# Audio tower on one core: a shared down product in three rounded products, routed weights loaded in place, gate and up in banks of their own, and 99 blocks

## The chip, the core and the metric

The kernel runs on one core of a Trainium2 chip. The metric is the device time of one execution in microseconds. A core has five engines with a queue each: PE (TensorE, matrix products; its loads of stationary operands are PEld), DVE (VectorE), ACT (ScalarE), POOL (GpSimd) and SP (SyncE, which issues DMA transfers). Engines run their own queue in order and wait for each other through semaphores.

## What is computed

The reference takes x of 16 sequences, 128 channels and 750 times. Three layers follow each other:

```python
# tokenizer: forward and backward moving average over time, then a projection 128 -> 256
ewma = (scan(x) + reversed_scan(x)) * 0.5
h = einsum('btc,dc->btd', ewma, W) + b
# two selective scans of 64 states along time
delta = softplus(x @ Wd + bd); u = x @ Wi + bi
h_t = exp(-delta * softplus(A_log)) * h_(t-1) + delta * u;  y = h_t @ Wo + bo
hidden = y + state @ Ws + bs
# mixture of experts over 12000 tokens: 16 experts in 4 groups of 4; each token keeps 2 groups, 4 experts
shared = (silu(x @ sg.T) * (x @ su.T)) @ sd.T                      # hidden size 512
routed = sum_e w_e * ((silu(x @ gate_e) * (x @ up_e)) @ down_e)    # 64 per expert
```

The scans are linear, and the kernel folds some weights into each other ahead of time. float32 accuracy is kept by splitting an operand into a rounded part (fp32r, "hi") and a rest ("lo") and adding three products: hi by hi, hi by lo and lo by hi.

## The kernel before

**Iterations and ticks.** The sequences are worked on in 8 pairs, one iteration each, of 24 ticks (`TICKS`), and a tail of 22 ticks. A tick holds one slot: a shared slot (`SHARED`: ticks 0 to 3, 7 to 10, 13 to 16) or a block slot (`ROUTED`: ticks 4 to 6, 11, 12, 17 to 23). Iteration q works the shared slots of pair q, and the blocks of tokens up to pair q-1. I call ticks 0 to 16 stretch A and ticks 17 to 23 stretch B of an iteration; B has seven block slots and no shared one.

**A shared slot** takes 500 tokens and a quarter of the shared hidden size. PE makes gate and up (12 products 500 wide, `shared_products`, L1593), ACT takes silu of gate (L868), DVE multiplies by up (`shared_hidden`, L1388), and three ticks later PE makes the down product (`shared_down`, L1656) in plain float32: 4 products in 8 records. After four such slots DVE adds the sum to the rows (`finish`, L1404).

**A block slot** takes 128 tokens that chose the same two groups. POOL gathers them through a list (L734), PE transposes them (L1635, `block_x`), ACT and DVE split them (L880, L1408), and PE makes gate and up (`block_products`, L1616): for each of the two groups six products 512 wide, gate in the first half of a bank and up in the second. ACT takes silu of both at once (`block_silu`, L873), after all twelve. DVE multiplies by up and by the weight of the token, one expert at a time (`block_hidden`, L1397, eight instructions 64 wide). PE transposes the result (L1643), ACT and DVE split it again (L891, L1414), PE makes the down product in 12 products 256 wide (`block_down`, L1674), ACT copies the sum (L886) and POOL adds it to the output (L745).

**Lists of blocks.** A block needs 128 tokens of one class of two groups. After the first pair only 6 full blocks are sure to be there, but 12 slots are run; entries without a token are masked by their index. The loop makes `KB` = 12 blocks in each of seven iterations and `KE` = 22 in the tail, 106 in all.

**The chain** (`CHAIN`) is the work that leads a pair from x to its lists: the moving average (`ewma`, scans L1038 and L1045, then POOL L690 and L692), projection (`tok`, L1511), layer statistics, the two scans (`pre`, `ssm_*`; L829, L831 and L834 on ACT, L1110 on DVE), the parts of the state (`split`, L1115), the class row (L1123), residuals on POOL (L706), `y` (PE L1558, DVE L1137), second statistics (L1066 to L1074), transposes, router (L1567), lists and the table of blocks (`table`, L1355 to L1378). Each step names a tick for each engine, counted from tick 0 of its pair: DVE=-30.5 of pair q is tick 17.5 of iteration q-2. An event at a whole tick runs before the tick's block or shared work on ACT and DVE, one at a half in the middle of the tick. `PREPARE` holds the loading and folding of weights in the same way. Chain, block inputs and block hidden rows use two banks in turn (`ch_ps`), in the order in which PE comes to them.

**Order in a tick** before, on ACT: silu of the block one slot back, sum of the block four back (L886), input of the next block (L880), chain, silu of this shared slot, chain, hidden rows of the block two back (L891). On DVE: the shared product one slot back, the rest of the next block's input (L1408), `finish`, chain, the block's hidden rows one slot back, chain, the rest of the block two back (L1414).

**Buffers** that the change touches: `h_tok` and `h2` (rows of the pair ahead of `y` and after it), four `hid` buffers, `fw` (the forward scan, and between times the scratch of the router), `block_rows` (8, and at the start the raw routed weights), `ws1` with a zero half per sequence.

## Time and profile before

| what | us |
|---|---|
| three runs | 1447.79, 1443.96, 1449.68 (median 1447.79) |
| the profiled execution | 1445.21, its span 1443.4 |
| PE busy in the span | 1221.5 |
| DVE busy | 997.5 |
| ACT busy | 559.2 |
| POOL busy | 599.7 |

The profile lists what each engine did in one execution. A busy PE isn't PE at its full pace, since products overlap: what counts is the distance from one start to the next. The granted clock of PE was 0.916 of full speed over the span.

### The profile page before, as it was taken

Reading aid. Unit: us, or ns where it says so; the run is one execution under the profiler, and the core shown is the slowest. Engines: PE = TensorE matmul, PEld = TensorE weight load, DVE = VectorE, ACT = ScalarE, POOL = GpSimd, SP = SyncE. Lnnn points to the kernel's source line nnn. Section 1 sums busy time; section 2 is a strip of 40 time slices with the busy share of each in tenths; the row PEclk is TensorE's granted clock in tenths of the full one; section 3 lists DMA queues with packets and bytes.
Section 4 is the critical chain, followed back from the end, with each engine's and each line's share of the span. In section 5 each row is a group of like instructions: output and inputs, shape, how many; then the busy total and the mean of one; then the engine's idle time right before and its main releaser. Section 6 shows DMA issues by size and latency. Waiting matters only on the chain.

```text
span 1443.4 us, 22785 instructions
## 1 busy us (share of the span) xinstructions
PE 1221.5 (85%) x6476; PEld 1036.5 (72%) x6476; DVE 997.5 (69%) x2991; ACT 559.2 (39%) x925; POOL 599.7 (42%) x442
## 2 busy tenths in 40 slices
PE   4439948996899779996799879998699979999997
PEld 3328736884788658885688658886588868888886
DVE  6785895779548875779548885588647774665553
ACT  1523613651336423551235423463236523323332
POOL 2261163155422743146332635138341553265553
PEclk9559978998899999998899978998899999999999
DMA  3601112221221112221231112212122213123330
GB/s 73 154 27 58 32 25 79 48 45 37 39 71 41 32 43 56 68 43 33 47 81 41 32 37 43 70 38 42 37 63 49 46 42 69 40 37 58 48 36 9
DMA packets 86891, 71.00 MB, mean 49 GB/s; under 512 B 38654, under 2 KB 81471, under 8 KB 86776
## 3 DMA queue, kind: packets, MB, share of 16 engines
q0 software_dynamic: 23616, 25.52, 11.6%
q1 hardware_dynamic: 60928, 43.61, 10.6%
q8 instruction: 62, 1.02, 0.3%
q10 hardware_dynamic: 2232, 0.42, 0.2%
q14 instruction: 53, 0.43, 0.1%
HBM read 33.10 MB, written 39.52 MB: 50 GB/s over the span
## 4 chain that ended last, share of the span: by engine, by line
PE 56%; DVE 25%; issue 10%; POOL 3%; DMA 3%; ACT 2%; POOLq 0%; DVEq 0%; SPq 0%; ACTq 0%
PE gu_ps L1616 14%; PE gu_ps L1593 13%; PE d_ps L1674 9%; PE d_ps L1656 6%; DVE hid L1397 5%; PE ch_ps L1567 3%; PE ch_ps L1511 2%; PE ch_ps L1643 2%; DVE h L1404 1%; DVE h L1137 1%; DVE fw L1038 1%; DVE states L1115 1%; PE ch_ps L1635 1%; PE ch_ps L1521 1%; DVE ends L1030 1%
## 5 line engine op out<-in xcount | busy, mean ns | idle before, releaser
L745 POOL DMA_INDIRECT out_dram<-block_rows,entry x106 | 171.7, 1620 | 328.2 <-ACT block_rows L886 173.0
L1616 PE MATMUL gu_ps<-gu_hi,bx_hi 128*128 x424 | 193.0, 455 | 12.8 <-issue 12.7
L713 POOL DMA_INDIRECT lists<-listed,pos x96 | 131.8, 1373 | 164.7 <-DVE pos L1307 140.2
L1656 PE MATMUL d_ps<-down,hid 128*125 128x256 f32 x768 | 191.6, 395 | 0.0
L1397 DVE SCALAR_TENSOR_TENSOR hid<-gu_ps,entry,hid 128x64 f32<-128x64 f32 x848 | 171.7, 276 | 8.0 <-ACT hid L873 7.1
L1616 PE MATMUL gu_ps<-gu_hi,bx_lo 128*128 x424 | 176.1, 415 | 0.0
L1616 PE MATMUL gu_ps<-gu_lo,bx_hi 128*128 x424 | 175.4, 414 | 0.0
L1656 PEld LDWEIGHTS d_ps<-down,hid 128*125 128x125 f32 x768 | 147.9, 198 | 22.8
L873 ACT ACTIVATE hid<-gu_ps 128x512 f32<-128x512 f32 x106 | 63.4, 598 | 231.9 <-PE gu_ps L1616 231.8
L734 POOL DMA_INDIRECT block_rows<-token_rows,entry x106 | 112.5, 1061 | 64.5 <-issue 35.5
L1408 DVE TENSOR_TENSOR bx_lo<-ch_ps,bx_hi 128x256 fp32r<-128x256 f32 x106 | 44.6, 421 | 131.5 <-ACT bx_hi L880 127.9
L1674 PE MATMUL d_ps<-dr_hi,hid_hi 128*128 x424 | 125.8, 297 | 6.5 <-DVE h L1404 6.4
L891 ACT ACTIVATE hid_hi<-ch_ps 128x512 fp32r<-128x512 f32 x106 | 63.3, 597 | 151.6 <-PE ch_ps L1643 149.4
L1674 PE MATMUL d_ps<-dr_lo,hid_hi 128*128 x424 | 120.4, 284 | 0.0
L1674 PE MATMUL d_ps<-dr_hi,hid_lo 128*128 x424 | 119.9, 283 | 0.0
L1616 PEld LDWEIGHTS gu_ps<-gu_hi,bx_hi 128*128 128x128 f32 x424 | 85.3, 201 | 31.8 <-issue 18.8
L1414 DVE TENSOR_TENSOR hid_lo<-ch_ps,hid_hi 128x512 fp32r<-128x512 f32 x106 | 72.6, 685 | 47.8 <-ACT hid_hi L891 47.8
L1616 PEld LDWEIGHTS gu_ps<-gu_lo,bx_hi 128*128 128x128 f32 x424 | 85.1, 201 | 21.2
L1616 PEld LDWEIGHTS gu_ps<-gu_hi,bx_lo 128*128 128x128 f32 x424 | 85.9, 203 | 12.6
L868 ACT ACTIVATE hid<-gu_ps 128x500 f32<-128x500 f32 x96 | 56.2, 589 | 91.8 <-PE gu_ps L1593 90.8
L1674 PEld LDWEIGHTS d_ps<-dr_hi,hid_hi 128*128 128x128 f32 x424 | 81.0, 191 | 10.7 <-issue 9.0
L886 ACT ACTIVATE block_rows<-d_ps 128x256 f32<-128x256 f32 x106 | 40.8, 385 | 121.0 <-PE d_ps L1674 121.0
(273 smaller groups left out, 3006.8 us busy)
## 6 DMA issues: line engine op xcount, KB each, us to landing
token_rows<-xn SPq DMA_DIRECT2D x24, 500.0 KB
out_dram<-h SPq DMA_DIRECT2D x24, 500.0 KB
t<-rstd_scratch SPq DMA_DIRECT2D x24, 250.0 KB, 4.0
x_in<-in_x_dram SPq DMA_DIRECT2D x15, 375.0 KB, 3.4
entry<-lists SPq DMA_DIRECT2D x106, 8.0 KB, 2.5
block_rows<-token_rows,entry POOLq DMA_INDIRECT x106, 2.8
out_dram<-block_rows,entry POOLq DMA_INDIRECT x106, 3.8
lists<-listed,pos POOLq DMA_INDIRECT x96, 2.7
```

Of the source, the lines that this page charges most:

```text
L713: pool.indirect_dma_start(out=lists, out_offset=bass.IndirectOffsetOnAxis(pos[:, arg:arg + 1], 0), in_=listed[:, arg, :], in_offset=None). ...
L734: pool.indirect_dma_start(out=block_rows[u], out_offset=None, in_=token_rows[0:there, :], in_offset=bass.IndirectOffsetOnAxis(entry[n % UE ...
L745: pool.indirect_dma_start(out=out_rows[0:there, :], out_offset=bass.IndirectOffsetOnAxis(entry[n % UE][:, ID:ID + 1].bitcast(U32), 0), in_ ...
L868: inc(act.activation(hid[g % 4][:, 0:TT], gu_ps[:, 2 * (g % 2), 0:TT], ACT.Silu), "silu_done")
L873: inc(act.activation(hid[g % 4].rearrange("p (g h) -> p g h", g=2), gu_ps[:, 2 * (g % 2):2 * (g % 2) + 2, 0:GH], ACT.Silu), "silu_done")
L891: inc(act.activation(hid_hi[g % 2][:], ch("bh", 0, n), ACT.Copy), "b_hi")
L1397: last = dve.scalar_tensor_tensor(h, up, entry[n % UE][:, e:e + 1], h, ALU.mult, ALU.mult)
L1414: inc(dve.tensor_tensor(hid_lo[g % 2][:], ch("bh", 0, n), hid_hi[g % 2][:].bitcast(F32), ALU.subtract), "b_lo")
L1593: last = pe.matmul(bank, w[:, k, ms], xx[:, k, :], start=(k == 0 and q == 0), stop=(k == KD - 1 and q == 2))
L1616: last = pe.matmul(gu_ps[:, 2 * (g % 2) + q, :], a[n % 2][:, k, :], w[:, k, bass.ds(of, 1), :].rearrange("p g h -> p (g h)"), start=(k == ...
L1656: last = pe.matmul(d_ps[0:TP, j, :], hid[g % 4][:, tc], down[:, m, :], start=(m == 0 and j % 2 == 0), stop=(m == M - 1), skip_group_check= ...
L1674: last = pe.matmul(d_ps[:, 2 * (n % 2), :], a[g % 2][:, m * P:(m + 1) * P], rows_[:, bass.ds(of, 1), half * D:(half + 1) * D].rearrange("p ...
```

## The change

- **99 blocks.** The iterations take 0, 6, 12, 12, 11, 12, 12 and 12 blocks, and the tail 22. The slots that come free (ticks 4, 5, 6, 11, 12 and 17 of iteration 1, tick 4 of iteration 4) hold chain steps only.
- **Shared down** in 12 products 256 wide of `hid_hi`, `hid_lo`, `down_hi` and `down_lo`. ACT makes `hid_hi` (`shared_hi`) and DVE `hid_lo` (`shared_lo`, both of its inputs in SBUF) at the end of the tick two after the slot's own, and `shared_down` waits for that.
- **Banks.** Block gate goes to one bank and block up to another, in 24 products 256 wide. ACT takes silu in the slot's own tick, once gate is there. DVE multiplies up by the weights, in its bank (one instruction 512 wide), and then `hid` by that (one more).
- **ACT's order:** the next block's input first, then the sum, the chain and silu.
- **Routed weights** go from DRAM straight to the place of their lower part; their split moves from ticks ahead of tick 0 to ticks 1.4 to 11.4 of iteration 0.
- **Buffers.** Rows are kept in one of two `h` by parity, in place; three `hid`, six `block_rows`, and `route_t` for the router's scratch; three waits on `fw` fall away. `ws1` is half as large.
- **ACT tables** for Exp are loaded ahead of the waits of `ssm_log` and `ssm_decay`.
- **Ticks.** Most steps have other ticks, and `EARLY` gives nine of them others in iterations 0 and 1.

```diff
-    ("ewma", 0, dict(SP=-32.0, DVE=-30.5, POOL=-29.0, ACT=-28.5)),
-    ("ewma_back", 0, dict(DVE=-29.5)),
+    ("ewma", 0, dict(SP=-32.0, DVE=-33.5, POOL=-29.0, ACT=-28.5)),
+    ("ewma_back", 0, dict(DVE=-32.0)),
...
-    (-16.4, "routed", 0),
+    (1.4, "routed", 0),
...
-    taken = 0
     for q in range(1, NP):
-        taken = min(taken + KB, full(q))
-    KE = (B * T - NCLS) // P + NCLS - taken
-    NB = KB * (NP - 1) + KE
+        first.append(first[-1] + take[-1])
+        take.append(min(KB, full(q) - first[q]))
+    first.append(first[-1] + take[-1])
+    KE = (B * T - NCLS) // P + NCLS - first[NP]
...
+                    act.preload_act_table(ACT.Exp)
...
-            def block_silu(g):
-                wait(act, "prod_mm", done(g))
+            def silu(g, n):
+                wait(act, "half_mm", done(g))
                 hidden_is_free(g)
-                inc(act.activation(hid[g % 4].rearrange("p (g h) -> p g h", g=2),
-                                   gu_ps[:, 2 * (g % 2):2 * (g % 2) + 2, 0:GH], ACT.Silu), "silu_done")
+                inc(act.activation(hid[g % 3][:, 0:n], gu_ps[:, 2 * (g % 2), 0:n], ACT.Silu), "silu_done")
+
+            def shared_hi(pair, n, g):
+                wait(act, "hid_done", done(g))
+                wait(act, "down_mm", done(g - 2))
+                inc(act.activation(hid_hi[g % 2][:, 0:TT], hid[g % 3][:, 0:TT], ACT.Copy), "s_hi")
...
-                if slot(g - 1)[0] == "B":
-                    block_silu(g - 1)
+                if slot(g + 1)[0] == "B":
+                    block_x(slot(g + 1)[1], g + 1)
...
-                for e in range(2 * EG):
-                    h = hid[g % 4][:, e * H:(e + 1) * H]
-                    up = gu_ps[:, 2 * (g % 2) + e // EG, GH + e % EG * H:GH + (e % EG + 1) * H]
-                    last = dve.scalar_tensor_tensor(h, up, entry[n % UE][:, e:e + 1], h, ALU.mult, ALU.mult)
-                inc(last, "hid_done")
+                up = gu_ps[:, 2 * (g % 2) + 1, :].rearrange("p (e h) -> p e h", h=H)
+                if part == 0:
+                    wait(dve, f"entry_in{n % UE}", 16 * (n // UE + 1))
+                    wait(dve, "prod_mm", done(g))
+                    w = entry[n % UE][:, 0:2 * EG].unsqueeze(2).broadcast_to([P, 2 * EG, H])
+                    inc(dve.tensor_tensor(up, up, w, ALU.mult), "up_weighed")
+                else:
+                    h = hid[g % 3].rearrange("p (e h) -> p e h", h=H)
+                    wait(dve, "up_weighed", n + 1)
+                    wait(dve, "silu_done", done(g))
+                    inc(dve.tensor_tensor(h, h, up, ALU.mult), "hid_done")
...
+            def shared_lo(pair, n, g):
+                wait(dve, "s_hi", s_count(pair, n))
+                inc(dve.tensor_tensor(hid_lo[g % 2][:, 0:TT], hid[g % 3][:, 0:TT], hid_hi[g % 2][:, 0:TT].bitcast(F32),
+                                      ALU.subtract), "s_lo")
...
-                wait(pe, "hid_done", done(g))
+                wait(pe, "s_lo", s_count(pair, n))
...
-                    last = pe.matmul(d_ps[0:TP, j, :], hid[g % 4][:, tc], down[:, m, :],
-                                     start=(m == 0 and j % 2 == 0), stop=(m == M - 1), skip_group_check=True)
+                    for q, (a, w) in enumerate(((hid_hi, down_hi), (hid_hi, down_lo), (hid_lo, down_hi))):
+                        last = pe.matmul(d_ps[0:TP, j, :], a[g % 2][:, tc], w[:, m, :],
```

On DVE, around tick 17 of iteration 4, before: the last rows of the table of blocks, the parts of the state (`states`), the moving average of the pair two ahead (`ends`, and the scan that writes `fw`), and the first `y` (the row that writes `h`).

```order
922 L1378 TENSOR_SCALAR table<-fw 1x12
923 L1115 TENSOR_TENSOR states<-t,states 64x750 x2
924 L1030 TENSOR_SCALAR ends<-x_in 128x2
925 L1038 SCALAR_TENSOR_TENSOR fw<-c,ends,x_in 128x750
926 L1408 TENSOR_TENSOR bx_lo<-ch_ps,bx_hi 128x256
927 L1137 TENSOR_TENSOR h<-ch_ps,h_tok 125x512
928 L1143 BN_STATS stats<-h 125x6 x2
929 L1397 SCALAR_TENSOR_TENSOR hid<-gu_ps,entry,hid 128x64 x8
930 L1045 SCALAR_TENSOR_TENSOR x_in<-c,ends,x_in 128x750
```

The same place now:

```order
961 L1136 TENSOR_TENSOR states<-t,states 64x750 x2
962 L1384 TENSOR_TENSOR route_t<-route_t,step_c 1x66
963 L1386 TENSOR_REDUCE route_t<-route_t 1x11
964 L1387 TENSOR_SCALAR table<-route_t 1x11
965 L1384 TENSOR_TENSOR route_t<-route_t,step_c 1x66
966 L1386 TENSOR_REDUCE route_t<-route_t 1x11
967 L1387 TENSOR_SCALAR table<-route_t 1x11
968 L1427 TENSOR_TENSOR hid_lo<-hid,hid_hi 128x500
969 L1406 TENSOR_TENSOR gu_ps<-gu_ps,entry 128x512
970 L1421 TENSOR_TENSOR bx_lo<-ch_ps,bx_hi 128x256
971 L1152 TENSOR_TENSOR h<-ch_ps,h 125x512
```

The states now stand ahead of the table's last six rows (five more of the table stand a tick earlier), both scans have left for ticks 14.5 and 16, and a shared `hid_lo` and the product by the weights have come in.

On ACT, at ticks 20 and 21 of iteration 4, before: silu of a block (`hid`), the sum of an older one (`block_rows`), and the input of the next (`bx_hi`).

```order
470 L891 ACTIVATE hid_hi<-ch_ps 128x512
471 L873 ACTIVATE hid<-gu_ps 128x512
472 L886 ACTIVATE block_rows<-d_ps 128x256
473 L880 ACTIVATE bx_hi<-ch_ps 128x256
474 L852 ACTIVATE x_hi<-ch_ps 128x500
```

And now:

```order
504 L910 ACTIVATE hid_hi<-ch_ps 128x512
505 L899 ACTIVATE bx_hi<-ch_ps 128x256
506 L905 ACTIVATE block_rows<-d_ps 128x256
507 L888 ACTIVATE hid<-gu_ps 128x512
508 L872 ACTIVATE x_hi<-ch_ps 128x500 x2
```

The input of the next block has moved ahead of the sum and of silu.

## Rows read from the trace of the kernel before

**Rows 1.** Windows by tick: stretch, length, busy time (instructions), clock, DMA.

```profile
core 0: us, PE busy (x) PEld busy (x) DVE busy (x) ACT busy (x) POOL busy (x), PEclk, DMA share, GB/s
0.00:119.60 119.60, 51.82 (x206) 42.98 (x207) 92.36 (x204) 37.45 (x48) 43.62 (x34) 0.66 0.34 79
119.60:181.40 61.80, 59.31 (x288) 49.32 (x288) 45.15 (x140) 33.94 (x45) 9.44 (x7) 0.97 0.16 47
181.40:232.90 51.50, 25.61 (x120) 22.14 (x119) 43.12 (x91) 9.23 (x16) 30.63 (x22) 0.67 0.13 32
232.90:319.90 87.00, 84.33 (x453) 71.64 (x451) 61.49 (x202) 47.52 (x71) 25.64 (x21) 1.00 0.23 59
319.90:394.10 74.20, 56.06 (x272) 45.62 (x271) 55.56 (x141) 17.79 (x34) 38.40 (x28) 0.84 0.19 41
725.20:816.70 91.50, 89.36 (x498) 76.89 (x496) 63.29 (x209) 49.44 (x76) 30.87 (x23) 1.00 0.25 55
816.70:892.50 75.80, 56.50 (x272) 46.50 (x271) 55.62 (x141) 17.79 (x34) 38.45 (x28) 0.84 0.19 40
1149.80:1201.70 51.90, 43.30 (x236) 35.50 (x235) 37.00 (x123) 15.39 (x31) 29.63 (x24) 0.97 0.20 42
1321.20:1423.60 102.40, 102.40 (x629) 89.11 (x629) 54.21 (x213) 39.02 (x84) 51.66 (x39) 1.00 0.30 41
```

**Rows 2.** Chain that ended last, in the tail: start, us, what.

```profile
1419.11 1.40 PE gu_ps L1616 x6
1420.51 0.44 PE ch_ps L1643 x4
...
1422.34 1.44 PE d_ps L1674 x12
```

**Rows 3.** The same chain in stretch A of iteration 4, a shared down.

```profile
744.97 1.73 PE d_ps L1656 x8
```

**Rows 4.** Groups by form, whole span: count, busy us, mean ns, idle before.

```profile
L1397 DVE SCALAR_TENSOR_TENSOR hid<-gu_ps,entry,hid 128x64 f32<-128x64 f32 x848 | 171.7, 276 | 8.0 <-ACT hid L873 7.1
L1414 DVE TENSOR_TENSOR hid_lo<-ch_ps,hid_hi 128x512 fp32r<-128x512 f32 x106 | 72.6, 685 | 47.8 <-ACT hid_hi L891 47.8
L891 ACT ACTIVATE hid_hi<-ch_ps 128x512 fp32r<-128x512 f32 x106 | 63.3, 597 | 151.6 <-PE ch_ps L1643 149.4 <-issue 2.1
L1102 DVE TENSOR_TENSOR t<-t 128x750 f32<-128x750 f32 x16 | 15.0, 935 | 1.9 <-ACT t L831 1.1
```

**Rows 5.** DVE's timeline in stretch B of iteration 4.

```profile
818.58 2.19 DVE L1367 TENSOR_TENSOR fw<-kth,upto_b 1x72 f32<-1x72 f32 x1
...
823.51 1.90 DVE L1115 TENSOR_TENSOR states<-t,states 64x750 fp32r<-64x750 f32 x2
825.44 2.63 DVE L1030 TENSOR_SCALAR ends<-x_in 128x2 f32<-128x2 f32 x1
828.11 1.78 DVE L1038 TENSOR_TENSOR_SCAN fw<-c,ends,x_in 128x750 f32<-128x750 f32 x1
...
839.97 3.38 DVE L1074 TENSOR_TENSOR mv<-halves 125x4 f32<-125x4 f32 x1
```

**Rows 6.** POOL's timeline in the same stretch.

```profile
818.80 1.87 POOL L706 TENSOR_TENSOR h_tok<-h_tok,rows 125x512 f32<-125x512 f32 x1
...
825.53 2.50 POOL L706 TENSOR_TENSOR h_tok<-h_tok,rows 125x512 f32<-125x512 f32 x2
...
840.82 2.49 POOL L706 TENSOR_TENSOR h_tok<-h_tok,rows 125x512 f32<-125x512 f32 x2
```

**Rows 7.** Who waited for whom, whole span: us, times, longest.

```profile
DVE bx_lo L1408 <- ACT bx_hi L880: 127.9, 58, 4.9
```

**Rows 8.** Chain that ended last, stretch B of iteration 0.

```profile
213.84 7.18 DMA out_dram<-h
```

**Rows 9.** The same chain ahead of tick 0.

```profile
46.22 1.28 ACT L829
...
54.75 3.85 DVE t L1110
...
64.27 5.13 DMA hid<-L_ffn_shared_down_w_dram
```

More of the change, by code:

```diff
@@ new lines @@
+    ("class_row", 0, dict(PE=-7.0, DVE=-7.5)),
+    ("residual", 4, dict(POOL=-2.5)),
+    ("split", (1, 1), dict(ACT=-6.0, DVE=-7.0)),
+    ("residual", 5, dict(POOL=-2.0)),
+    ("y", (0, 0), dict(PE=-5.5, DVE=-6.0)),
+    ("y", (0, 1), dict(PE=-5.0, DVE=-4.5)),
+    ("ln2_stats", 0, dict(DVE=-4.5, POOL=-4.5)),
+    ("y", (1, 0), dict(PE=-4.5, DVE=-4.5)),
+    ("ln2_norm", 0, dict(DVE=-3.5, ACT=-3.5)),
+    ("y", (1, 1), dict(PE=-4.0, DVE=-4.0)),
+    ("ln2_norm", 1, dict(DVE=-1.5, ACT=-0.5)),
@@ new lines @@
+    ("table", 0, dict(DVE=15.0)),
+    ("list", 10, dict(POOL=19.5)),
+    ("table", 1, dict(DVE=16.5)),
+    ("table", 2, dict(DVE=16.5)),
+    ("route_weights", 0, dict(DVE=13.0)),
+    ("table", 3, dict(DVE=17.5)),
+    ("list", 11, dict(POOL=20.0)),
+)
+EARLY = {
+    (1, "tok", 5): dict(DVE=-24.5),
+    (1, "table", 3): dict(DVE=19.5),
+    (1, "list", 11): dict(POOL=22.0),
+    (1, "list", 6): dict(POOL=16.5),
+    (0, "route_top", 0): dict(DVE=10.5),
+    (0, "route_groups", 1): dict(DVE=7.5),
+    (0, "route_marks", 0): dict(DVE=12.0),
+    (1, "list", 8): dict(POOL=19.5),
+    (1, "table", 0): dict(DVE=14.0),
+}
@@ L144 @@
+    (11.4, "routed", 5),
+    (-7.7, "shared", 5),
+    (-9.5, "routed_loads", 0),
+    (-8.5, "routed_loads", 1),
+    (-7.5, "routed_loads", 2),
+    (-6.5, "routed_loads", 3),
+    (-5.5, "routed_loads", 4),
+    (-4.5, "routed_loads", 5),
 )
@@ L582, in prepare @@
                                      w.rearrange("(m p) c -> p m c", p=P)).then_inc(S[f"w_shared{n}"], 16)
-                    for n in range(3):
-                        routed_chunk(n)
-                elif what == "routed" and 1 <= n <= 3:
-                    routed_chunk(n - 1 + 3)
+                elif what == "routed_loads":
+                    load_routed(n)
                 elif what == "shared" and n == KD:
@@ L709, in chain @@
                     if arg == 0 and pair:
-                        for n in range(KB * (pair - 1), KB * pair):
+                        for n in range(first[pair], first[pair + 1]):
                             wait(pool, f"entry_in{n % UE}", 16 * (n // UE + 1))
@@ L725, in fetch @@
                 u = n % U
-                if n % KB == 0:
+                if n == first[iteration[n]]:
                     for t in range(NT):
@@ L739, in add_to_out @@
                 u = n % UO
-                if n % KB == 0:
+                if n == first[iteration[n]]:
                     for t in range(NT):
@@ L832, in chain @@
                 elif step == "ssm_decay":
+                    act.preload_act_table(ACT.Exp)
                     wait(act, "delta_done", 2 * pair + arg + 1)
@@ L1336, in blocks_from @@
                 last = pair == NP - 1
-                n0, k = KB * pair, KE if last else KB
+                n0, k = first[pair + 1], take[pair + 1]
                 fl, got, many, by = tb
@@ L1578, in banks_of_slot @@
             def banks_of_slot(g):
-                if slot(g)[0] == "S" and slot(g - 2)[0] == "S":
-                    wait(pe, "silu_done", done(g - 2))
-                else:
-                    wait(pe, "hid_done", done(g - 2))
+                wait(pe, "silu_done", done(g - 2))
             def shared_products(pair, n, g, amid, groups):
```

385 lines of the change are left out of this document (184 added, 201 removed).

## The prediction

> **What bounds the kernel now.** I read the windows first [rows 1], cut at the first gate product of a tick; the cuts fall at the ends of stretches A and B, so that every row is one kind of work. Three regimes are to be seen. In the tail 21 block slots take 102.40 us, 4.88 each, and PE is busy for all of it at full clock: PE is the bound. In stretch A of iteration 4 (twelve shared and five block slots) PE is busy for 89.36 of 91.50 us, again the bound, and DVE has 63.29 of work, so a cover of 28. In stretch B PE is busy for only 56.50 of 75.80 us, at a clock of 0.84, and DVE for 55.62: seven block slots, 34 us at the tail's pace, take 76. Neither is full; they wait for each other through the chain. Without averages and projection for a pair two ahead, as in iteration 6, the same stretch takes 51.90 us. Ahead of tick 0 lie 119.60 us in which DVE is busy for 92.36, and iteration 0, which has no blocks, takes 61.80 and 51.50.
>
> Then the chain and the timelines. DVE's rows in B [rows 5] tell why the first `y` is late: the table, from 818.58 to the states at 823.51, then `ends` and a scan from 825.44 to 829.89. Three rows there are far longer than their size: 2.19 us for 72 numbers, 2.63 for two columns, 3.38 for four columns. Each lies over a residual of POOL [rows 6] and ends with it. Last, the waits [rows 7]: DVE waited for the block input from ACT 58 times, 127.9 us; ACT makes it behind silu of the previous block and a sum.
>
> **The change part by part**, against the profiled execution's 1445.2 us. That lies 2.6 below the median of the runs, which is inside their spread.
>
> *Six blocks of iteration 1.* Five leave ticks 4 to 12. Iteration 1 takes 87.00 there, and iteration 0, which has the same chain steps and no blocks, 61.80 [rows 1]: -25. The sixth leaves tick 17, a block at the tail's 4.88: -5. Together -30; at least -18, if the chain waits as long without them. One more leaves iteration 4: -5.
>
> *Shared down.* Eight records take 1.73 us [rows 3]; twelve products 256 wide take 1.44 in a block's down [rows 2], with the same stationary loads. That is -0.29 for each of 96. All lie in stretch A, where PE sets the pace, but iteration 0's are on a chain of waits, so 84 count: -24.
>
> *Block gate and up.* Twelve products 512 wide take 2 x 1.40; 24 of 256 take 2 x 1.44 [rows 2]: +0.08 for each of 99, +8.
>
> *Stretch B of iterations 1 to 5.* Ahead of the first `y` the table (4.9) and `ends` with its scan (4.4) go, and two `hid_lo` come, each of 500 columns where 750 take 935 ns [rows 4], 0.62: -8.1. The scan back, of the same length as the 1.78 [rows 5], leaves a tick in which PE waits too, and I count half: -0.9. ACT's order takes one silu out from ahead of each block input, a pass of 512 columns as the 597 ns of row L891: seven times 0.6, -4.2. `block_hidden` takes 171.7 / 106 = 1.62 now and should take twice one pass of 512 from a bank, 0.685 [rows 4], 1.37: seven times, -1.7. The sum is -14.9, and I take -14, which leaves 62 us: five times, -70. Below that, the stretch can't go under seven slots and its own chain on PE, for which I take the 56.5 it is busy now, part of it at half clock: -19. Above, half of it, -7, if the waits only change places. Iteration 6 has no scans there: -6.
>
> *Stretch A with more for DVE and ACT.* DVE gets twelve `hid_lo` (7.4), two scans (3.6), and some 1.5 of table, 12.5 us a stretch; ACT gets twelve passes of 0.59, 7.1 on 49.44. The 28 us of DVE's cover shrink to about 13 of the 88 that PE then needs. Queued behind `hid_lo` on DVE is the next tick's shared product and so PE's banks; behind the new wait of `shared_down` on PE stands the whole next slot. I charge +3 for each of seven iterations, +21; nothing at the low end, +8 each at the high end.
>
> *Ahead of tick 0.* The splits of the routed weights leave. Now they hold up the load of the shared down weights (5.13 us, behind a buffer wait of SP) and lie over a scan that takes 3.85 on DVE; an Exp table of 1.28 sits on the chain twice [rows 9] and goes ahead of the wait. Of this sum, 5.1 + 2.0 (a scan of the same 750 columns takes 1.78) + 2.6, I take all, -10. No row shows what a direct load costs while it lies beside the pair's rows; its bounds are nothing and its own 5.13.
>
> *Iteration 0.* `y` waits for a transfer of 7.18 us, since `h2` must be stored first [rows 8]; with two `h` it doesn't: -7. Two Exp loads, -2.6. Against it come the six splits on ACT and POOL and `hid_lo`: +3. Together -7.
>
> *At nothing:* `ws1` by halves (one more wait of PE in a step that occurs once a pair), six `block_rows` (gathered up to six slots ahead), three `hid`, whose third is needed free one slot sooner: all hidden by the slot's other work as long as DVE is not a whole tick late; 1 us a pair if it is.
>
> The sum: -30 - 5 - 24 + 8 - 70 - 6 + 21 - 10 - 7 = -123, so 1322 in a profiled execution and 1325 as a median.
>
> **A rule that speaks against the change.** Row by row, three instructions of DVE were held by a residual of POOL for about 2, 2.5 and 3.2 us [rows 5, 6]. `shared_lo` reads two operands from SBUF, where a block's rest reads one from PSUM; two of them per iteration come at ticks 17 and 18, where residuals start at tick 17.5. If each is held for a pair of residuals, 2.5 us, that is +5 in each of seven iterations, and on the chain.
>
> The Trainium skill's page "SBUF — State Buffer", section "SBUF: two separate sides", says just this: a DVE instruction with two inputs in SBUF and a GpSimd instruction that reads SBUF lock each other out for a whole instruction. The trace agrees as far as the three rows go.
>
> **The rivals.**
>
> 1. *DVE becomes late (rival).* The lock costs the 35 us above, or stretch A +8 instead of +3, also 35: 1360, and with half the gain in B 1395. For it: DVE would be busy for 76 of 88 us in A, and PE now waits for DVE in every slot instead of in block slots only. Against: the residuals run in stretch B, and A has little of POOL but transfers. Chance 0.22.
> 2. *Stretch B falls to PE's own work.* 56.5 instead of 62 in five iterations, -27, and A pays nothing, -21: 1277. For it: iteration 6 does it at 51.90. Against: averages and projections stay, and the three held rows may stay too. Chance 0.18.
> 3. *The new ticks do nothing.* Only the seven blocks leave and the rest cancels: 1448 - 35 = 1413. Chance 0.06.
> 4. *Slower: `shared_down` waits for DVE.* PE's queue stops at the end of each tick until DVE has ended the tick before. Everything else saves 123 + 21 = 144 us, so 84 shared slots would have to lose 1.7 us each to bring the kernel back to where it was, and 1.8 for slower by over 0.5%. DVE's slack is 13 us over 17 ticks, 0.8 a tick, and for a loss of 1.8 a tick it would have to be late almost always. Chance 0.04, at 1460.
>
> The forecast itself, 1300 to 1355, has 0.5. About 0.5% is what a measurement of this kernel can tell from no change. Faster by more than that is 0.95, the same 0.02, slower 0.03. The range takes in the cases 1 and 2 with their bounds: 1270 to 1390.
>
> **What would show it.** Iteration 1 shorter by 30 or more; tail slots at 4.96 instead of 4.88; the shared down at 1.44 and not 1.73; stretch B of iterations 2 to 5 at 62; stretch A at 88 to 94, with DVE at 76 in it; two instructions of 0.68 in place of eight; the block input no longer first among DVE's waits; tick 0 at 110. Wrong would be: a stretch A over 97 (rival 1 or 4, told apart by whether DVE or PE's wait for `s_lo` is long), a B under 57 (rival 2) or over 70 (rival 3), or 256-wide products that take more than 0.12 us from start to start in the new order.

## The result, and the profile after

Four runs of the changed kernel gave 1388.3 to 1393.0 us, median 1389.8; four of the kernel before beside them gave 1447.4. The ratio is 0.961, with a 95% interval of 0.958 to 0.963: 4% faster, where 8.5% was forecast. Windows with the same cuts and columns as [rows 1]: ahead of tick 0, iteration 0, A and B of iteration 1, A and B of 4, B of 6, 21 slots of the tail.

```profile
0.00:106.10 106.10, 50.33 (x206) 42.41 (x207) 82.65 (x197) 33.28 (x43) 25.44 (x27) 0.66 0.37 90
106.10:230.50 124.40, 93.33 (x455) 80.32 (x454) 100.86 (x243) 56.76 (x79) 53.77 (x32) 0.78 0.13 38
230.50:307.20 76.70, 64.98 (x351) 54.65 (x350) 63.06 (x182) 44.38 (x62) 19.40 (x12) 0.93 0.16 46
307.20:366.80 59.60, 44.60 (x315) 42.23 (x314) 42.08 (x85) 15.50 (x30) 26.95 (x21) 0.86 0.13 33
684.40:774.20 89.80, 84.54 (x551) 75.56 (x549) 69.45 (x193) 51.56 (x81) 35.37 (x25) 0.98 0.27 61
774.20:838.00 63.80, 51.17 (x368) 48.74 (x368) 45.96 (x94) 18.67 (x36) 33.91 (x24) 0.89 0.18 38
1090.60:1143.10 52.50, 42.72 (x331) 40.52 (x331) 34.19 (x75) 16.73 (x33) 23.60 (x19) 0.97 0.16 35
1266.70:1370.80 104.10, 104.10 (x882) 104.10 (x882) 48.30 (x84) 38.57 (x83) 50.10 (x38) 1.00 0.30 44
```

Against [rows 1]: 13.5 less ahead of tick 0, 11 more in iteration 0 (113.3 there), 10 and 15 less in the stretches of iteration 1, 12 less in B of iteration 4. A of iteration 4 lost a block and only 1.7 us (b_99, the kernel before with 99 blocks, loses 0.9 there). A tail slot is 104.10 / 21 = 4.96, where it was 4.88. The waits of the changed kernel that have to do with new code:

```profile
ACT hid L888 <- DVE hid_lo L1427: 59.7, 24, 4.1
DVE hid_lo L1427 <- ACT hid_hi L893: 39.7, 23, 4.1
DVE h L1152 <- POOL h L725: 25.4, 6, 6.0
PE d_ps L1684 <- DVE hid_lo L1427: 23.6, 10, 5.8
PE d_ps L1703 <- DVE h L1417: 19.6, 9, 2.8
```

The wait of [rows 7] is out of the first places. New are waits for `hid_lo` of a shared slot (L1427), and one of DVE for POOL's residual (L1152 for L725).

### The profile page after: what moved, and what is told of

The parts are those of the page before. It is cut to its first block, busy times and chain, and to the rows that moved or that the text cites. A ratio compares the mean times of both kernels' runs of the same rounds, so it can differ in the third digit from the quotient of the medians.

```text
span 1389.0 us, 25702 instructions
## 1 busy us (share of the span) xinstructions
PE 1170.6 (84%) x7838; PEld 1073.6 (77%) x7838; DVE 981.0 (71%) x2424; ACT 591.6 (43%) x989; POOL 590.9 (43%) x428
## 4 chain that ended last, share of the span: by engine, by line
PE 48%; issue 17%; DVE 16%; POOL 12%; ACT 3%; DMA 3%; SPq 1%; POOLq 0%; DVEq 0%; ACTq 0%
PE gu_ps L1642 14%; PE gu_ps L1617 9%; PE d_ps L1703 9%; POOL lists L732 5%; PE ch_ps L1594 3%; PE d_ps L1684 3%; POOL block_rows L753 3%; PE ch_ps L1533 2%; PE ch_ps L1670 2%; POOL h L725 2%; PE ch_ps L1543 1%; DVE fw L1054 1%; POOL out_dram L764 1%; PE ch_ps L1662 1%; DVE hid_lo L1427 1%
## 5 line engine op out<-in xcount | busy, mean ns | idle before, releaser
L888 ACT ACTIVATE hid<-gu_ps 128x512 f32<-128x512 f32 (+1 forms) x195 | 115.3, 592 | 368.2 <-PE gu_ps L1642 226.8
L1642 PE MATMUL gu_ps<-gu_hi,bx_hi 128*128 x792 | 240.3, 303 | 14.5 <-issue 14.5
L1642 PE MATMUL gu_ps<-gu_lo,bx_hi 128*128 x792 | 230.9, 292 | 0.0
L1642 PEld LDWEIGHTS gu_ps<-gu_hi,bx_hi 128*128 128x128 f32 x792 | 157.7, 199 | 23.4 <-issue 22.8
L1642 PEld LDWEIGHTS gu_ps<-gu_hi,bx_lo 128*128 128x128 f32 x792 | 157.9, 199 | 0.4
L1642 PEld LDWEIGHTS gu_ps<-gu_lo,bx_hi 128*128 128x128 f32 x792 | 157.2, 199 | 0.0
L1684 PE MATMUL d_ps<-down_hi,hid_hi 128*125 128x256 f32 x384 | 118.1, 308 | 23.9 <-DVE hid_lo L1427 23.6
L1684 PE MATMUL d_ps<-down_hi,hid_lo 128*125 128x256 f32 x384 | 112.1, 292 | 0.0
L1684 PE MATMUL d_ps<-down_lo,hid_hi 128*125 128x256 f32 x384 | 111.9, 291 | 0.0
L1684 PEld LDWEIGHTS d_ps<-down_hi,hid_hi 128*125 128x125 f32 x384 | 75.8, 197 | 31.4 <-DVE hid_lo L1427 31.1
L1427 DVE TENSOR_TENSOR hid_lo<-hid,hid_hi 128x500 fp32r<-128x500 f32 x96 | 70.2, 731 | 40.6 <-ACT hid_hi L893 39.7
```

What stands on the lines that cost most here:

```text
L888: inc(act.activation(hid[g % 3][:, 0:n], gu_ps[:, 2 * (g % 2), 0:n], ACT.Silu), "silu_done")
L1427: inc(dve.tensor_tensor(hid_lo[g % 2][:, 0:TT], hid[g % 3][:, 0:TT], hid_hi[g % 2][:, 0:TT].bitcast(F32), ALU.subtract), "s_lo")
L1642: last = pe.matmul(gu_ps[:, 2 * (g % 2) + half, q * GH:(q + 1) * GH], a[n % 2][:, k, :], w[:, k, bass.ds(of, 1), half * GH:(half + 1) * GH ...
L1684: last = pe.matmul(d_ps[0:TP, j, :], a[g % 2][:, tc], w[:, m, :], start=(m == 0 and q == 0 and j % 2 == 0), stop=(m == M - 1 and q == 2), ...
```

## The experiments

Three theories for what was missing stood at the start. Theory 1: POOL's queue holds up stretch B. Theory 2: POOL's splits of the routed weights, moved into iteration 0, hold DVE there. Theory 3: the new waits for `hid_lo` and the DVE instruction behind them. The rival to all is that the terms were wrong in size and no new wait matters.

Eighteen kernels were run in five groups, each with its own runs of the kernel before (medians 1445.8 to 1450.0), so ratios compare best. "C" is the changed kernel with both product edits undone.

| kernel | median us | ratio to before | 95% interval |
|---|---|---|---|
| changed | 1389.8 | 0.961 | 0.958-0.963 |
| b_99: before, 99 blocks | 1424.4 | 0.984 | 0.981-0.986 |
| a_down32: changed, float32 shared down | 1369.4 | 0.947 | 0.946-0.949 |
| a_banks_old: changed, old block gate/up | 1376.4 | 0.951 | 0.949-0.953 |
| a_both = C | 1355.5 | 0.937 | 0.932-0.941 |
| a_pe_no_lo | 1380.9 | 0.954 | 0.950-0.959 |
| a_hid_free | 1388.7 | 0.960 | 0.955-0.964 |
| a_no_lo | 1369.3 | 0.942 | 0.939-0.946 |
| a_pool_first | 1409.1 | 0.974 | 0.971-0.976 |
| a_pool2 | 1411.3 | 0.975 | 0.971-0.980 |
| c_oldchain | 1432.3 | 0.986 | 0.982-0.991 |
| c_scans_back | 1369.0 | 0.942 | 0.937-0.946 |
| c_tables_back | 1359.6 | 0.940 | 0.938-0.942 |
| c_y_back | 1425.3 | 0.985 | 0.983-0.987 |
| c_ssm_back | 1372.7 | 0.947 | 0.944-0.950 |
| c_routed_back | 1357.4 | 0.934 | 0.931-0.938 |
| a_lists_back | 1362.3 | 0.942 | 0.938-0.946 |
| c_lists_back | 1337.9 | 0.924 | 0.923-0.926 |
| c_lists_late | 1321.7 | 0.912 | 0.909-0.915 |

Lengths from the profiled executions, cut as above; each column adds up to its span. The profiled executions of a_down32 and C are 5 and 3 us faster than their medians.

| stretch | before | b_99 | changed | a_down32 | C | c_lists_late |
|---|---|---|---|---|---|---|
| ahead of tick 0 | 119.6 | 121.1 | 106.1 | 106.2 | 104.8 | 105.4 |
| iteration 0 | 113.3 | 116.3 | 124.4 | 113.8 | 112.3 | 116.2 |
| iteration 1 | 161.2 | 136.5 | 136.3 | 124.1 | 126.6 | 122.0 |
| A of 2 to 5 | 365.5 | 365.4 | 369.1 | 363.1 | 360.6 | 362.2 |
| B of 2 to 5 | 299.5 | 296.1 | 260.2 | 260.5 | 257.9 | 236.6 |
| iteration 6 | 142.6 | 147.6 | 147.1 | 146.5 | 143.0 | 138.0 |
| iteration 7 | 119.4 | 119.8 | 123.5 | 125.6 | 124.1 | 120.4 |
| tail | 122.2 | 121.6 | 122.3 | 122.3 | 120.6 | 121.5 |

**99 blocks alone.** The edit is `take.append(min(KB, full(q) - first[q]))` and what follows from it.

> The kernel before with 99 blocks instead of 106 and nothing else of the change. The prediction gives -30 for iteration 1 and -5 for iteration 4: 1412, ratio 0.976. The changed kernel's iteration 1 came out only 24.9 us shorter, though other edits also act there. If the chain waits as long without blocks, iteration 1 gives -18 and the kernel 1424 (0.984). A result near 1412 says that the terms of the blocks were right and that what is missing lies elsewhere.

1424, the number of the lower bound, but not by its mechanism: iteration 1 is 24.7 shorter and not 18, 14 in A and 11 in B, and iteration 4 another 3. Of this 5 come back in iteration 6 and 3 in iteration 0.

**The two product edits, one by one and together.** The cuts show the products alone; silu, DVE's instructions and ACT's order of a block go back with them in a_banks_old, the buffers in a_down32.

```diff
 a_down32
-        for q, (a, w) in enumerate(((hid_hi, down_hi), (hid_hi, down_lo), (hid_lo, down_hi))):
-            last = pe.matmul(d_ps[0:TP, j, :], a[g % 2][:, tc], w[:, m, :], ...)
+        last = pe.matmul(d_ps[0:TP, j, :], hid[g % 4][:, tc], down[:, m, :], ...)
 a_banks_old
-        last = pe.matmul(gu_ps[:, 2 * (g % 2) + half, q * GH:(q + 1) * GH], ...)
+        last = pe.matmul(gu_ps[:, 2 * (g % 2) + q, :], ...)
```

> The changed kernel with before's plain float32 shared down (eight instructions, no rounded part and no rest, four hid buffers, one down load). By the prediction it loses 0.29 us for each of 96 shared slots on PE and gets back the charge of 3 us for each stretch A: about +24 - 21, 1393. Theory 3 (DVE and ACT carry the new rest too late, PE waits for hid_lo in every shared slot): 1365 to 1380, with stretch A at or under 90. Theory 1 (POOL's queue is what keeps stretch B long) expects B unchanged at 64 to 65 and the kernel at 1390 to 1410.

> The changed kernel with before's gate and up of a block: products 512 wide into two banks, silu after all twelve, eight DVE instructions a block that read entry and both halves, and the wait for DVE ahead of the products. The prediction puts this edit at -2.9 for each of five stretches B on the chain (-14), another -3 a stretch for ACT's order, and +8 for PE's narrower products: undoing it gives about 1390 + 30 - 8, 1412. If the order of ACT and DVE in a block hides all of it, the undone edit gives -8, 1382.

> The changed kernel with both product edits undone: plain float32 shared down with four hid buffers, and before's 512-wide block gate and up. One alone gave 1369.4 and the other 1376.4, where the changed kernel stands at 1389.8, so 20.4 and 13.4 were lost to them. If the two losses are of different places (the first in iterations 0 and 1, the second in stretches A and in the tail), they add: 1356. If both are the same wait for DVE seen twice, the second undoing gives little: 1366 or more.

Both undoings make the kernel faster, by 20.4 and 13.4 us, and they add: 1355.5 where 1356 was expected. Theory 3 holds for the first. The table above says where that loss lies: 10.6 in iteration 0, 12.2 in iteration 1, 6 in the four stretches A, none in B. The second lies elsewhere. Up to 8 of its 13.4 are the width, as forecast (4.96 a tail slot and not 4.88), and between the profiled executions of a_down32 and C, 3.5 us lie in iteration 6, 2.5 each in the stretches A and B of 2 to 5, 1.7 in the tail. PE's timeline in A of iteration 3 says why the twelve narrow products saved nothing. First the changed kernel, then the eight float32 products of a_down32: the first start of the down, and the start of the next product.

```profile
600.23 0.39 PE L1684 MATMUL d_ps<-down_hi,hid_hi 128*125 128x256 f32 x1
...
601.75 0.39 PE L1617 MATMUL gu_ps<-x_hi,gate_hi 128*128 128x500 f32 x1
...
608.50 0.36 PE L1703 MATMUL d_ps<-dr_hi,hid_hi 128*128 x1 [2.83 <-DVE h L1417]
```

```profile
574.39 1.89 PE L1681 MATMUL d_ps<-down,hid 128*125 128x256 f32 x8
...
575.93 0.58 PE L1615 MATMUL gu_ps<-x_hi,gate_hi 128*128 128x500 f32 x1
...
580.36 0.36 PE L1699 MATMUL d_ps<-dr_hi,hid_hi 128*128 x1 [0.93 <-DVE h L1417]
```

From start to start a shared down takes 1.52 as three rounded products and 1.54 in float32; over all slots after iteration 1 the medians are 1.50 and 1.54. The 1.73 of [rows 3] is a duration up to the end of the last product, which overlaps the next one's start. In the kernel before, the same down of iteration 4 starts at 744.80 and what follows at 746.34, 1.54 later too:

```profile
744.80 1.89 PE L1656 MATMUL d_ps<-down,hid 128*125 128x256 f32 x8
746.34 0.59 PE L1616 MATMUL gu_ps<-gu_hi,bx_hi 128*128 x1
```

The third row of each of the two timelines shows PE waiting for DVE's `finish` in the same place, 2.83 against 0.93: PE is no longer what sets the end of this tick. The windows of that A, of the changed kernel and of a_down32, agree: PE is busy for 2 us less and the stretch is longer.

```profile
527.20:620.20 93.00, 88.08 (x594) 79.04 (x592) 70.88 (x195) 53.13 (x85) 35.85 (x26) 1.00 0.28 61
```

```profile
500.60:592.40 91.80, 90.06 (x558) 79.85 (x556) 66.17 (x188) 48.35 (x75) 36.53 (x25) 1.00 0.28 62
```

**Which part of the shared rest costs.** Three kernels take away one piece each.

```diff
 a_pe_no_lo
-                wait(pe, "s_lo", s_count(pair, n))
+                wait(pe, "s_hi", s_count(pair, n))
-  ((hid_hi, down_hi), (hid_hi, down_lo), (hid_lo, down_hi))
+  ((hid_hi, down_hi), (hid_hi, down_lo), (hid_hi, down_hi))
 a_hid_free
-                    wait(act, "s_lo", s_count(*was[1:]))
+                    wait(act, "s_hi", s_count(*was[1:]))
-                inc(dve.tensor_tensor(hid_lo[...], hid[...], hid_hi[...], ALU.subtract), "s_lo")
+                inc(dve.tensor_tensor(hid_lo[...], hid_hi[...], hid_hi[...], ALU.subtract), "s_lo")
 a_no_lo: the edits of both but for the last, and no shared_lo on DVE
```

> The changed kernel, where PE's third product of a shared down reads hid_hi once more and not hid_lo, and waits for ACT's hid_hi alone; DVE still computes hid_lo. So the product with the rest of the hidden is left out, at the same count and width of instructions. If PE's wait for DVE at the end of a tick is what costs the 20 us of the split shared down: 1370 to 1375. If it is DVE's time (0.67 a slot), or ACT's wait for DVE ahead of silu (a third hid buffer where four were): 1385 to 1390, unchanged.

> The changed kernel, where DVE's hid_lo of a shared slot is hid_hi minus hid_hi, so that hid is free once ACT has rounded it and silu of the slot three later doesn't wait for DVE; the rest of the hidden is thereby left out (it is zero), with DVE's and PE's instructions and PE's wait as they were. If ACT's wait for DVE ahead of silu (59.7 us, 24 times in the changed kernel) costs the 20 us: 1370 to 1375. If PE's own wait or DVE's time does: 1385 to 1390.

> The changed kernel without any hid_lo of a shared slot: DVE doesn't compute it, PE's third product reads hid_hi once more, ACT and PE wait for ACT's hid_hi alone. So the product with the rest of the hidden is left out; PE's count and width of instructions and ACT's work are as in the changed kernel. PE's wait for hid_lo alone gave 9 of the 20.4 us (1389.8 to 1380.9). If the rest is DVE's time, 0.67 in each of 96 slots: 1370 or less. If the rest is ACT's rounding pass and its place in ACT's queue: 1380.

ACT's wait, the longest in the list of waits, is worth nothing (0.960, inside the changed kernel's interval). PE's wait is worth 9 us, and DVE's instruction another 12, which brings the kernel to a_down32's 1369. That the two agree is in part chance: in the profiled execution of a_no_lo iteration 7 is 10 us longer than in the changed kernel, nearly all of it in B, so elsewhere it gains 31. The gaps of PE's weight loads for which the profile shows no wait are 8.0 us there and 4.5 in the changed kernel; the reason is open, so the 12 for DVE's instruction is a net figure. How the wait works is to be seen in the chain of the changed kernel in iteration 0:

```profile
152.44 2.25 DVE route_t L1292
...
155.02 0.93 DVE states L1136
...
156.48 0.93 DVE states L1136
...
157.44 0.69 DVE hid_lo L1427
158.18 2.92 PE d_ps L1684 x12
```

And the first two of the twelve in PE's timeline:

```profile
158.18 0.58 PE L1684 MATMUL d_ps<-down_hi,hid_hi 128*125 128x256 f32 x1 [5.79 <-DVE hid_lo L1427]
158.55 0.41 PE L1684 MATMUL d_ps<-down_lo,hid_hi 128*125 128x256 f32 x1
```

`hid_lo` stands at the end of DVE's tick, behind routing and `states`. PE has waited 5.79 us for it, with the whole next tick queued behind the down, and then takes 2.72 from start to start (2.92 to the end of the last), where it took 1.52 in stretch A. The products lie 0.21 apart there and 0.12 in stretch A, and the granted clock of these 2.72 us was 0.50, the lower of its two levels (1.2 of 2.4 GHz):

```profile
158.18:160.90 2.72, 2.72 (x13) 2.72 (x14) 1.15 (x9) 0.00 (x0) 0.00 (x0) 0.50 0.00 0
```

So PE came out of its wait at the lower level. In iterations 0 and 1 of a_down32 the granted clock is 0.84 and 0.94, in the changed kernel 0.78 and 0.90 (A and B of iteration 1: 0.93 and 0.86):

```profile
106.20:220.00 113.80, 89.76 (x408) 74.43 (x407) 93.79 (x231) 50.44 (x67) 51.26 (x32) 0.84 0.14 42
220.00:344.10 124.10, 107.84 (x616) 93.29 (x615) 93.64 (x254) 53.10 (x80) 44.65 (x32) 0.94 0.16 45
```

No run separates how much of the 23 us in these two iterations is the clock and how much the waits themselves.

**POOL's order, first try.** In stretch B of the changed kernel the first `y` waits for POOL's residuals, and they stand behind list transfers. I moved them up, and the first sum of averages with ACT's copy of it; in a_pool2 ACT's stays at -28.5.

```diff
-    ("ewma", 0, dict(SP=-32.0, DVE=-33.5, POOL=-29.0, ACT=-28.5)),
+    ("ewma", 0, dict(SP=-32.0, DVE=-33.5, POOL=-31.0, ACT=-30.5)),
-    ("residual", 0..2, dict(POOL=-6.5)),
+    ("residual", 0..2, dict(POOL=-7.0)),
```

> The changed kernel with POOL's order altered in two places alone: the first sum of averages (fw plus scan back) and ACT's copy of it 2 ticks earlier, and the first three residuals ahead of the list transfers 5 to 8. Theory 1 (in stretch B the first y and the block of the scan both wait for POOL, which works off twelve list transfers, gathers and adds without a gap): each of five stretches B falls by 3 to 6 us, 1360 to 1375, and POOL's share of the chain falls from 12% to under 8%. Rival (DVE and the two-way chain of PE and DVE keep B long, POOL is only the last one seen): within 5 us of 1390.

> The changed kernel with POOL's order altered alone (first sum of averages at -31, first three residuals ahead of the list transfers 5 to 8). The run before it had also moved ACT's copy of the averages ahead of ACT's copy of the states, and DVE then waited 9.5 us for the states in every stretch B. Theory 1: without that the first y no longer waits 3.15 us for POOL and the averages' transfer starts some 6 us earlier; each of five stretches B falls by 3 to 6 us, 1362 to 1376. Rival (the chain of DVE and PE sets the pace of B, POOL's place in it is taken by the next wait): 1385 to 1395.

Both lost about 20 us, and theory 1 seemed to fall. The rows of a_pool2 in B of iteration 4, POOL and then DVE, show what happened:

```profile
787.21 4.32 POOL L725 TENSOR_TENSOR h<-h,rows 125x512 f32<-125x512 f32 x3
790.94 2.31 POOL L709 TENSOR_TENSOR fw<-fw,x_in 128x750 f32<-128x750 f32 x1
804.06 1.80 POOL L711 TENSOR_TENSOR ew_lo<-fw,ew_hi 128x750 fp32r<-128x750 f32 x1 [10.82 <-ACT ew_hi L816]
```

```profile
788.27 5.78 DVE L1136 TENSOR_TENSOR states<-t,states 64x750 fp32r<-64x750 f32 x1 [1.99 <-ACT states L836]
...
817.86 0.69 DVE L1152 TENSOR_TENSOR h<-ch_ps,h 125x512 f32<-125x512 f32 x1 [5.54 <-POOL h L725]
```

The step that I moved has two halves, and the second waits for ACT, which comes to it later: POOL stood still for 10.82 us with all else behind it, the fourth residual among it. And the residuals now lay beside DVE's `states`, which took 5.78 where it takes 0.94. In a_pool_first ACT had moved as well, ahead of its copy of the states, and in the same stretch DVE waited 9.51 us for that; its B of 2 to 5 is 262.5, only 2 more than in the changed kernel, and most of its loss lies in the stretches A (6), ahead of tick 0 (4) and in iteration 0 (5), which I didn't follow up. These trials moved more than the one thing, and don't settle whether POOL holds up B. The lists, tried last, do.

**Where the rest of the gain comes from.** b_99 to C is 69 us that no product edit explains.

```diff
 c_oldchain: CHAIN of the kernel before, EARLY empty. The others put back one group of it:
 c_scans_back    ("ewma", 0): DVE=-33.5 -> -30.5;  ("ewma_back", 0): DVE=-32.0 -> -29.5
 c_tables_back   ("table", 0..3): DVE=15.0, 16.5, 16.5, 17.5 -> 16.0, 16.0, 17.0, 17.0; its two rows of EARLY
 c_y_back        ("y", (2, 0)): PE=-1.5 -> -3.0;  ("y", (2, 1)): PE=-0.5 -> -2.0;
                 ("logit", 0): PE=-2.0 -> -1.5; ln2_stats, ln2_norm, x2t and
                 the other y by 0.5 to 1.5 ticks
 c_ssm_back      pre, split, carry, ssm_*, class_row, spread
```

> On the same kernel (1355.5), the whole table of chain steps of the kernel before, so that what stays of the change is the 99 blocks, the routed weights loaded in place, two h buffers, six block_rows, ws1 by halves. The kernel before with 99 blocks alone stands at 1424. The prediction's terms for the table are -9.0 in five stretches B and -6 in iteration 6, and for the loads and the buffers -10 and -7: about 1406 if each is what I took it for. If the loads and buffers give all of the 69 us: 1360; if they give nothing: 1424.

> On the kernel with both product edits undone (1355.5), the scans of batch 0 (ends, scan, scan back) at their ticks of the kernel before, in stretch B ahead of the first y. The prediction gave 4.4 + 0.9 us of each of five stretches B to these two moves: 1355.5 + 26, 1382. Rival (the first sum of averages waits for POOL's place in its own queue, so the scan's tick is free within B): 1350 to 1362.

> On the kernel with both product edits undone (1355.5), the four table steps alone at their ticks of the kernel before (16, 16, 17, 17). The prediction gave the table's 4.9 us ahead of the first y to each of five stretches B: 1355.5 + 25, 1380, all of it in B. Rival (as with the scans, DVE has the time there, since the first y waits for POOL's residual): 1352 to 1362.

> On the same kernel, the steps y, second norm with its statistics, x2t and logit at their ticks of before. The prediction costed their moves at nothing. If the order around y is what shortened stretch B, by 9 us each: 1355.5 + 40, about 1395. If not, within 7 of 1355.

> On the same kernel, the projections, splits, carry, state scan with its logarithm and decay, class row and the spread of the norm's rows at their ticks of before. The prediction costed their moves at nothing. If they shortened B and the stretch ahead of tick 0: 1375 to 1400. If not, within 7 of 1355.

With the old table nothing is left of the 69: 0.986 stands beside 0.984 of b_99, one interval over the other. So the table of steps is worth 5.0% and loads and buffers nothing together: against b_99, c_oldchain has 9 less ahead of tick 0 and 9 more in iteration 0. Of the groups, the scans give 0.5% by the ratios, with intervals that overlap, and nothing in B of 2 to 5 (255.6 with them back, 257.9 in C). The steps of the table of blocks give 1.4 us in each of these B and take 5.6 in the first two iterations, where their two rows of `EARLY` went as well; together nothing that can be measured. Projections and splits give 1.1%, in iterations 0 and 1 and the stretches A; B would be 1 us shorter without their moves. The steps around `y` are worth nearly all: 4.8%. (The parts add up to more than 5.0%, since the lists, below, cost 1.2%; the ticks of routing, token projection and residuals weren't tried alone.) Iteration 3, A and B, of c_y_back and then of C:

```profile
532.20:624.70 92.50, 89.99 (x498) 76.57 (x496) 68.14 (x217) 49.28 (x76) 32.71 (x22) 1.00 0.25 55
624.70:700.40 75.70, 56.21 (x272) 46.79 (x272) 45.43 (x133) 17.74 (x34) 37.32 (x27) 0.84 0.21 45
```

```profile
499.10:590.10 91.00, 89.53 (x498) 76.78 (x496) 68.77 (x224) 49.32 (x76) 36.56 (x25) 1.00 0.26 56
590.10:655.00 64.90, 49.07 (x270) 41.65 (x271) 44.50 (x126) 17.34 (x34) 35.70 (x25) 0.89 0.20 46
```

DVE's work in B is the same to 1 us, and B differs by 10.8. The last third's `y` has left ticks 21 and 22 for 22.5 and 23.5, and its norm's statistics have left B for the next A, which doesn't grow (91.0 against 92.5). In c_y_back the two slots that start at ticks 21 and 22 take 14.7 and 13.5, in C 9.4 and 6.7, and the clock is 0.84 against 0.89.

**The routed weights.**

> On the same kernel (1355.5), loads and splits of the routed weights ahead of tick 0 as in the kernel before, still in place. The prediction gave 10 us ahead of tick 0 to their leaving, and charged 3 in iteration 0, part of it the splits: 1355.5 + 10 - 2, 1363. If POOL's splits of 2.5 us hold DVE's instructions in iteration 0 as row by row in the changed kernel's trace (six held, 1.2 to 4 us over their size): iteration 0 gets 8 to 12 us shorter and the kernel stays at 1353 to 1358.

1357.4, no difference that can be measured. The profile shows both halves: ahead of tick 0 8.1 more (112.9), iteration 0 4.2 less (108.1). So theory 2 is right in that the splits cost iteration 0 some 4 us and not the 8 to 12 expected; the rest of what they give ahead of tick 0 is not to be found in the kernel's time.

**POOL's lists.** Of the twelve transfers that write a pair's lists, eight stand 0.5 to 2.5 ticks earlier in the changed kernel, three where they stood and one (5) later. Four now share tick 17.5 with the first residuals, and stand ahead of them. Their three rows of `EARLY` go with them in these runs.

```diff
 a_lists_back, c_lists_back
-    ("list", 0..11): POOL=12.5 13 14 14 15.5 17.5 17.5 17.5 17.5 18.5 19.5 20
+    ("list", 0..11): POOL=15 15 15 15.5 15.5 16 18 18 18.5 18.5 19.5 21.5
 c_lists_late, on c_lists_back
+    ("list", 6..9): POOL=19.5
```

> On the same kernel, POOL's twelve list transfers alone at their ticks of before (15 to 21.5 and not 12.5 to 20). In the changed kernel POOL works without a gap in the middle of B and holds up the residuals for the first y. If that costs anything, later lists help B and the kernel gets to 1340 to 1352, unless the entries for the next iteration then come late (iteration 7, the tail). If the earlier lists are what shortened B: 1365 to 1395.

> The changed kernel with POOL's twelve list transfers alone at their ticks of the kernel before. On the kernel without the product edits this gave 17.6 us (1355.5 to 1337.9), since four transfers no longer stand ahead of the residuals that the first y waits for. If POOL's queue costs the changed kernel the same: 1372. If its stretch B is then held by the other chain, over the new hid_lo and ACT: 1380 to 1390.

> On the kernel without the product edits and with before's lists (1337.9), list transfers 6 to 9 one to one and a half ticks later still, behind the first sum of averages. That sum stood at 607.4 in iteration 3, behind four transfers of 1.5 each, and x's next transfer and the scan behind it. If the scan's start follows POOL, each of five stretches B gets 1 to 4 us shorter: 1320 to 1333. If DVE's own queue has caught up by then, or the entries of the next blocks come late for it: 1335 to 1345.

All three gain: 17.6 us on C, 27.5 on the changed kernel, and 16.2 more by the later four. In C, iteration 3, POOL does four transfers of 1.2 us with 0.3 between them, then the residuals, and DVE waits (POOL, then DVE):

```profile
597.59 1.23 POOL L732 DMA_INDIRECT lists<-listed,pos  x1 [0.31 <-issue]
...
602.11 1.19 POOL L732 DMA_INDIRECT lists<-listed,pos  x1 [0.30 <-issue]
603.33 3.71 POOL L725 TENSOR_TENSOR h<-h,rows 125x512 f32<-125x512 f32 x3
```

```profile
604.70 0.69 DVE L1160 TENSOR_TENSOR h<-ch_ps,h 125x512 f32<-125x512 f32 x1 [6.94 <-POOL h L725]
```

In c_lists_back the residuals come first, and the first `y` follows DVE's own work without a wait:

```profile
595.29 4.36 POOL L722 TENSOR_TENSOR h<-h,rows 125x512 f32<-125x512 f32 x3
```

```profile
602.30 0.67 DVE L1157 TENSOR_TENSOR h<-ch_ps,h 125x512 f32<-125x512 f32 x1
```

B of iterations 2 to 5 falls from 64 to 61 each on C, to 59 in c_lists_late, and from 65 to 59 on the changed kernel. Theory 1 holds after all, in the form: what stands in POOL's queue ahead of a step that DVE waits for. It explains 2% of the kernel's time on the changed kernel. For c_lists_late that step isn't the residual: in B of iteration 3 its first `y` comes 1.9 us later than in c_lists_back, but the sum of averages starts 9.7 us into the stretch instead of 15.8, and the scan behind it takes 1.78 instead of 3.72, as it no longer lies beside a residual. c_lists_late, with a ratio of 0.912, beats both kernels: 8.8% faster than before and 5% faster than the changed kernel.

## Why the prediction was right or wrong

The direction was right, the size half of it: 58 us and not 123. 1389.8 lies just inside the range, whose upper end, 1390, is below the 1395 that the prediction itself gives for the worse case of rival 1. Put together by what the runs can separate, its terms are -35 for the blocks, -68 for steps, loads and buffers (-9.0 in each of five stretches B, -6, -10, -7) and -20 for the two product edits (-24, +8, +21 and the other 25 of stretch B). Measured are -24, -69 and +34. So the step that failed is the price of the two product edits, off by 54 of the 65 us that are missing; and that the second group came out to 1 us is luck, for its terms were wrong one by one. Rival 1 gives a number near the measured one, but its mechanism isn't what happened: no stretch A grew by 8, and POOL held `shared_lo` for 4 us in all, not 35. By its own steps:

- **The blocks, -35.** Measured -24 (1.6%): 25 less in iteration 1 where 30 were forecast, 3 less in iteration 4, 5 more in iteration 6 and 3 in iteration 0. The row of iteration 0 was the wrong stand-in: A of iteration 1 is 72.8 without blocks, not 61.8.
- **Shared down, -24. This step failed twice.** Its size: 1.73 was read as the pace of eight products, and is 1.54 from start to start, so at best 0.04 a slot. Its consequence: it was charged only part of +3 a stretch, and costs 20 in all, 9 by PE's wait and 12 by DVE's time. The mechanism was my rival 4, "PE's queue stops at the end of each tick until DVE has ended the tick before", but not its spread: I priced it as a loss in every shared slot of the stretches A, and 23 of the 27 us by which the two profiled executions differ lie in iterations 0 and 1, where DVE is behind.
- **Gate and up, +8.** The width was right: 4.96 a tail slot, as forecast. The gains put with it in B (ACT's order -4.2, `block_hidden` -1.7 a stretch) didn't come: B of 2 to 5 is 260.5 with them (a_down32) and 257.9 without (C). The edit as a whole costs 13.4, up to 8 by the width and the rest in places that no run takes apart.
- **Stretch B, -70. Right in part by its sum, wrong in every term.** Measured against [rows 1] and its like: 67.5, 64.2, 63.8 and 64.7, 39 less over four iterations where I had 56, so the 62 of a stretch was nearly met, from the wrong terms. The table of blocks (in the -8.1) gives 1.4 in B, the two scans nothing (B is 0.6 shorter with them back), ACT and DVE's block order nothing. About 10 come from the steps around `y`, which I had costed at nothing. And 6 were lost to lists that I had not costed: I weighed where DVE's and PE's steps went, and not what POOL's were moved past.
- **Stretch A, +21.** It grew by 0.7, 1.3, 2.5 and 3.4 us against b_99 in iterations 2, 3, 5 and 6, 2 on average, and by 3.9 in iteration 1; in iterations 4 and 7 it shrank by 0.8 and 1.0. That is 10 in all seven. With the down at 0.5 less and the width at 0.4 more, it is a charge of 1.5 where I took 3. DVE is busy for 70.88 us in A of iteration 3, not 76.
- **Ahead of tick 0, -10, and iteration 0, -7.** -13.5 and +11. Of the first 8 are the splits, and 4 of them come back in iteration 0. The store of 7.18 us [rows 8] is out of the chain of iteration 0, yet the -7 isn't there: C, without the shared rest, takes 112.3, 1 less than before, and the shared rest costs 10.6 more.
- **The rule on two operands in SBUF** was priced at 35 for `shared_lo`. Its 96 instructions take 731 ns where a block's take 686, 4 us in all; so the hold falls on other instructions (below), not on this one.
- **What would show it.** The signs for the tail, tick 0, the two 0.68 and the wait of [rows 7] came true. The shared down at 1.50 and iteration 1 shorter by 24.9 didn't, and they were the ones that carried most of the sum. None of the signs of being wrong came either: the stretches A of 2 to 6 take 89.8 to 94.6, the stretches B of 2 to 5 63.8 to 67.5. No sign watched iteration 0, where 18 us were lost against the forecast.

What stays open: why c_tables_back is faster in iterations 0 and 1 by what it loses in B (its ticks and its two rows of `EARLY` went together), and which of the steps around `y` does it. Putting `y` back without x2t and logit wasn't tried, since their shared banks fix the order.

## What to carry to other kernels

Take the price of a run of products from the start of the first to the start of what follows, never from their end. When an edit moves a step into a queue, list what now stands ahead of the steps that others wait for, on every queue: here lists moved ahead of residuals and sums, four transfers of 1.5 us each among them, cost 27.5 us, more than either product edit. A group of steps moved by up to a tick and a half, out of the ticks where two engines wait for each other, was worth 4.8%; no product that was made cheaper gave anything. A new instruction at the end of a late engine's tick costs, however much that engine idles on average.
